# Ten codebook levels parted around block sums, and one square moved behind a bank's copy

## The chip, the cores and the metric

The kernel runs on one core of a Trainium2 chip. The metric is the device time in microseconds (us) from one launch; three timed runs of the kernel before gave 1450.16, 1450.33 and 1450.46 us, with a median of 1450.33. The profile comes from one further execution that took 1451.06 us. Its span, from the first to the last instruction, is 1449.3 us, so 1.8 us lie around the span.

## The reference

The input x has 64 rows of 32 tokens with 512 features. What matters here:

```
W = weights[condition]                      # one of 16 mixing matrices for each of the 64 rows
hidden = einsum('bct,bcd->bdt', x, W)
q = rms_norm(hidden @ Wq + bq, gq)          # 512 -> 4096, 32 heads of 128
k = rms_norm(hidden @ Wk + bk, gk)
v = hidden @ Wv + bv
x = x + softmax(q k^T / sqrt(128)) v @ Wo + bo      # attention within each row's 32 tokens
lora_delta = lora_B @ lora_A * 0.5
normalized = (weight + lora_delta) / exp(scale_log)          # 512 x 512, groups of 128
quantized = cb[searchsorted((cb[:-1] + cb[1:]) / 2, normalized)]   # 64 codes
w_eff = (quantized - normalized + normalized) * scale + lora_delta
x = x + mixture_of_8_low_rank_experts(x @ w_eff.T)
```

The norm needs the sum of squares of q and of k over all 4096 features of a token. The quantised weight is looked up without a table: for each of the 63 thresholds ("levels") it adds step[t] wherever normalized > threshold[t].

## The kernel before, in words

All products are float32 in quality, made from float32r parts: an operand is kept as a rounded part (hi) and a rest (lo), and a product is hi\*hi + hi\*lo + lo\*hi, three matmuls for each 128 rows of depth.

**The q and k stage** is the first half of the program and the only one that the change touches. For each of 32 heads it makes q and k for two halves of the tokens, so there are 64 instances, counted by s (head h = s // 2; N_QK = 64). An instance is one Strassen-like block product: seven products (`p1` to `p7` of the TensorE part, line 720) stand for eight. Each is 6 matmuls of 512 columns. The order on TensorE is p6(s), p5(s), p1(s+1), p7(s), the scores of the head before where s is even (128 small matmuls, line 848), p2(s+1), p4(s), p3(s). I call p3 the third product and p4 the fourth, by their numbers. p3(s) adds into the bank that p5(s) filled, and it may only start once the result k_hi has been read out of that bank.

**ScalarE** copies intermediate banks to SBUF (`keep_a1`, `keep_a2`, `keep_a3`, lines 1166, 1175, 1184), rounds the weights (`split_qk`, line 1105), squares each of the four results of an instance (`square`, lines 1196 and 1198), scales q (`gain`, line 1202) and copies p4's bank out as k_lo (line 1284). The bank of p4(s) is also the one of p1(s+2); p1(s+2) waits for `sq_ready` to reach `sq_k_lo(s)`, that is for the square which reads this bank. The count of `sq_ready` follows the order of the squares on ScalarE: q_lo, k_hi, k_lo, q_hi.

**VectorE** makes the four results of an instance as block sums of a bank and a kept copy: `block_11` (q_lo, line 1761), `block_22` (k_hi, line 1774), `block_12` (q_hi, line 1787), each 128x512. It makes the rests of the weights (`low_qk`, line 1623), copies the scores out (`keep_scores`, line 1746), and between them walks the levels of the codebook for the first half of the weight. One level is two instructions of 128x1024: a comparison (line 1727, into qm) and a sum into qf (line 1728). The function `levels_qk(s)` gives 1 level to instances 6 to 59, and 2 to instances 7, 13, 19, ..., 55. The first level of an instance stands ahead of `block_22(s)`, the second near its end, ahead of `block_12(s)`.

**GpSimd** adds the squares to their running sums (`add_square`, line 1526, 128x512; the first 8 squares go there directly) and forms sums of weight blocks (`add_qk`, lines 1477 to 1489, 128x256).

The order on every engine is the order in which the code is written; engines meet by semaphores alone. A helper `link` makes VectorE wait for its own instruction before it goes on. After this stage come the v stage (line 739), attention and output projection (lines 922 and 963), and the experts. The change leaves them as they are.

Of the kernel before, what the change touches and what calls it, by code (L numbers as in the profile page):

```python
# [8 lines left out]
ALU = mybir.AluOpType  # L9
# [71 lines left out]

def levels_qk(s):
    return 0 if s < 6 or s > 59 else 2 if s > 6 and s % 6 == 1 else 1


def levels_v(s):
# [25 lines left out]
def build(nc, x_nat, x_tr, cond_w, cond_idx, codebook, wqk, wv_in, wo_in, vecs, bo, w2, scale_log,  # L112
# [4 lines left out]
    with ExitStack() as ctx:  # L117
        def sb(name, shape, dt=F32):
            return ctx.enter_context(nc.sbuf_tensor(name, shape, dt))

        def sem(name):
            return ctx.enter_context(nc.semaphore(name))
# [9 lines left out]
        thr = sb("thr", [P, NCODE + 1])  # L132
        thr_t = sb("thr_t", [P, NCODE])
        step = sb("step", [P, NCODE])
# [29 lines left out]
        with ExitStack() as mem_a:  # L164
# [29 lines left out]
        blk = {(name, par): qk[:, (2 * i + par) * 512:(2 * i + par + 1) * 512]  # L194
               for i, name in enumerate(("q_lo", "q_hi", "k_lo", "k_hi")) for par in range(2)}
# [5 lines left out]
        qv = (qreg[:, 0:1024], accr[:, 0:1024])  # L201
        update = (qreg[:, 1024:2048], accr[:, 2048:3072])
        qf = (qreg[:, 2048:3072], accr[:, 1024:2048])
        qm = qreg[:, 3072:4096]
# [53 lines left out]
        def bank_a(s):  # L258
            return bank[4 - 4 * (s % 2)]
# [90 lines left out]
        c22_done = sem("c22_done")  # L350
# [57 lines left out]
        def sq_q_lo(s):  # L408
            return 4 * s + 1

        def sq_k_hi(s):
            return 4 * s + 2

        def sq_k_lo(s):
            return 4 * s + 3

        def sq_q_hi(s):
            return 4 * s + 4
# [4 lines left out]
        def sq_slot(count):  # L423
            return sqst[:, (count - 1 - SQ_DIRECT) % 3, :]

        def acc_of(kind, n):
            return acc[:, kind, n * CH:(n + 1) * CH]
# [659 lines left out]
        def _(act):  # L1087
# [100 lines left out]
            def square(count, kind, n, src, bias):  # L1188
                if count <= SQ_DIRECT:
                    dst = acc_of(kind, n)  # L1190
                else:
                    if count > SQ_DIRECT + 3:
                        act.wait_ge(acc_done, count - SQ_DIRECT - 3)
                    dst = sq_slot(count)
                if bias is None:
                    act.activation(dst, src, ACT.Square).then_inc(sq_ready, 1)  # L1196
                else:
                    act.activation(dst, src, ACT.Square, bias=bias, scale=1.0).then_inc(sq_ready, 1)

            def gain(name, s, ready):  # L1200
                q = blk[name, s % (3 if name == "q_lo" else 2)]
                act.activation(q, q, ACT.Copy, scale=vec[:, s // 2, 3:4]).then_inc(ready, 1)

            def last_q(s):

                act.wait_ge(c12_done, s + 1)
                square(sq_q_hi(s), 0, s % 2 + 2, blk["q_hi", s % 2], None)
# [40 lines left out]
            for s in range(N_QK):  # L1248
                if s >= 1:
                    keep_a2(s)  # L1250
                    last_q(s - 1)
                    gain("q_hi", s - 1, gq_hi)
                if s == 2:
                    split_qk(4, 2)
                if s == 1:
                    keep_a3(s)
                act.wait_ge(c11_done, s + 1)
                square(sq_q_lo(s), 0, s % 2, blk["q_lo", s % 3], None)
                gain("q_lo", s, gq_lo)
                h = s // 2  # L1260
                if s % 2 == 1 and h + 1 < H:
                    split_qk(6, h + 1)
                elif s % 2 == 0 and s >= 2:
                    split_qk(3, h)
                if s >= 2:
                    keep_a3(s)
                elif s == 0:
                    difference(3, 7)
                if s % 2 == 1 and h + 1 < H:
                    split_qk(7, h + 1)  # L1270
                if s == N_QK - 1:
                    split_v(5, 0)
                    split_v(6, 0)
                keep_a1(s + 1)
                if s == 0:
                    split_qk(1, 1)
                    difference(2, 4)
                    difference(3, 4)
                act.wait_ge(c22_done, s + 1)
                square(sq_k_hi(s), 1, s % 2 + 2, blk["k_hi", s % 2], None)  # L1280
                if s % 2 == 0 and s >= 2 and h + 1 < H:
                    split_qk(1, h + 1)
                act.wait_ge(p_done[4], s + 1)
                act.activation(blk["k_lo", s % 2], bank_a(s)[:, :], ACT.Identity, bias=vec[:, h, 1:2], scale=1.0)\
                   .then_inc(c21_done, 1)
                square(sq_k_lo(s), 1, s % 2, bank_a(s)[:, :], vec[:, h, 1:2])
                if s == 0:
                    split_qk(4, 1)
                elif s % 2 == 1:
                    if s > 1 and h + 2 < H:  # L1290
                        split_qk(4, h + 2)
                if s == N_QK - 2:
                    split_v(1, 0)
                    split_v(2, 0)
# [308 lines left out]
        def _(dve):  # L1603
            chained = [0]

            def link(ins):
                chained[0] += 1
                ins.then_inc(chain, 1)
                dve.wait_ge(chain, chained[0])
# [37 lines left out]
            def code_order(s, last):  # L1647
                while s >= last:
                    mid, low, high = thr[:, s:NCODE:2 * s], thr[:, 0:NCODE:2 * s], thr[:, 2 * s:NCODE + 1:2 * s]
                    link(dve.tensor_tensor(mid, mid, low, ALU.max))  # L1650
                    link(dve.tensor_tensor(mid, mid, high, ALU.min))
                    s //= 2
# [70 lines left out]
            def first_level(half):  # L1723
                link(dve.tensor_scalar(qf[half], qv[half], 0.0, cb[:, 0:1], ALU.mult, ALU.add))

            def level(half, t):
                link(dve.tensor_scalar(qm, qv[half], thr[:, t + 1:t + 2], step[:, t:t + 1], ALU.is_gt, ALU.mult))
                link(dve.tensor_tensor(qf[half], qf[half], qm, ALU.add))  # L1728

            def straight_through(half, steps=(0, 1)):  # L1730
                for step in steps:
# [92 lines left out]
            taken = 0  # L1824
            for s in range(N_QK):
                h = s // 2
                if s >= 2:
                    block_12(s - 1)
                if s == 2:
                    low_qk(4, 2)  # L1830
                if s == 3:
                    code_steps()
                if s == 4:
                    normalised(0)
                if s == 5:
                    code_order(NCODE // 2, NCODE // 8)
                if s == 2:
                    dve.wait_ge(t_lo, 16)
                    code_scales(0)
                if s == 6:  # L1840
                    first_level(0)
                if s == 60:
                    straight_through(0)
                if s == 61:
                    effective(0)
                if levels_qk(s):
                    level(0, taken)
                    taken += 1
                if s == 1:
                    block_22(s)  # L1850
                if s % 2 == 1 and h + 1 < H:
                    low_qk(6, h + 1)
                elif s % 2 == 0 and s >= 2:
                    low_qk(3, h)
                if s == N_QK - 1:
                    low_v(1, 0)
                    low_v(2, 0)
                if s >= 2:
                    block_22(s)
                if s % 2 == 0 and s >= 2:  # L1860
                    keep_scores(s // 2 - 1)
                if s % 2 == 1 and h + 1 < H:
                    low_qk(7, h + 1)
                if s + 1 < N_QK:
                    block_11(s + 1)
                if s == 3:
                    keep_update(0)
                    keep_update(1)
                    dve.wait_ge(ld_quant[0], 16)
                if s == 4:  # L1870
                    normalised(1)
                if s == 5:
                    code_order(NCODE // 16, 1)
                if levels_qk(s) == 2:
                    level(0, taken)
                    taken += 1
                if s == N_QK - 1:
                    low_v(5, 0)
                if s == 0:
                    low_qk(1, 1)  # L1880
                    block_12(s)
                    low_qk(4, 1)
                elif s % 2 == 1:
                    if s > 1 and h + 2 < H:
                        low_qk(4, h + 2)
                elif h + 1 < H:
                    low_qk(1, h + 1)
                if s == 2:
                    code_scales(1)
# [70 lines left out]
            taken = 0  # L1960
# [217 lines left out]
```

## Time and profile before

| | |
|---|---|
| median of 3 runs | 1450.33 us (1450.16 to 1450.46) |
| the profiled execution | 1451.06 us, span 1449.3 us |
| TensorE busy | 1444.4 us of the span, 14507 matmuls |
| VectorE, ScalarE, GpSimd busy | 1080.4, 726.0, 745.2 us |
| granted TensorE clock | 1.0 |
| line 720, the products of the q and k stage | 2688 matmuls, from 13.6 to 682.4 us |
| a level of the first half: comparison, sum | 1199 ns and 1650 ns on the mean, 63 of each |
| block_22 (line 1774) | 688 ns on the mean, 96 of them |

A busy TensorE only says that some matmul was under way. A late start shows there as a longer pair of matmuls or as a gap ahead of a weight load, which the profile lists on its own row as PEld. The chain that ended last is made of TensorE's work for 98%.

### The profile page before, as it was taken

What the parts mean: (1) busy time and instruction counts of PE and PEld (TensorE: products, weight loads), DVE (VectorE), ACT (ScalarE), POOL (GpSimd) and SP (SyncE); (2) the same over time, 40 slices, a digit from 0 to 9 for tenths busy, and PEclk for the clock granted to TensorE, in tenths of its full rate; (3) what the DMA queues carried; (4) which work ended last, traced back from release to release, by engine and by line L of the source; (5) the groups of instructions that cost most, each with busy time, mean ns of one, the idle gap of its engine ahead of it and who ended that gap; (6) DMA issues with size and microseconds to landing.
All of it is one profiled execution on the core that took longest, in us unless ns stands there. A gap on an engine that the chain in (4) does not pass through costs nothing.

```text
span 1449.3 us, 34721 instructions
## 1 busy us (share of the span) xinstructions
PE 1444.4 (100%) x14507; PEld 1200.5 (83%) x14507; DVE 1080.4 (75%) x1507; ACT 726.0 (50%) x1331; POOL 745.2 (51%) x530
## 2 busy tenths in 40 slices
PE   9999999999999999999999999999999999999999
PEld 8788888888888888888888888888888888888887
DVE  8787868687786877875478888867987667667663
ACT  7766676766766767677333333334432322222221
POOL 7568777777777877776345555514561111112100
PEclk9999999999999999999999999999999999999999
DMA  4211011110111011102443344447663334244230
GB/s 152 66 45 45 31 38 45 45 45 24 45 45 45 27 41 45 45 31 67 136 152 139 133 133 137 145 148 246 201 194 110 103 118 132 83 137 132 74 118 30
DMA packets 106989, 135.13 MB, mean 93 GB/s; under 512 B 6224, under 2 KB 89424, under 8 KB 106320
## 3 DMA queue, kind: packets, MB, share of 16 engines
q1 hardware_dynamic: 106400, 132.62, 27.7%
q8 instruction: 114, 1.87, 0.5%
q14 instruction: 43, 0.35, 0.1%
q10 hardware_dynamic: 432, 0.30, 0.1%
HBM read 86.75 MB, written 46.14 MB: 92 GB/s over the span
## 4 chain that ended last, share of the span: by engine, by line
PE 98%; DVE 1%; issue 0%; ACT 0%; DVEq 0%; POOL 0%; ACTq 0%; POOLq 0%
PE bank L720 41%; PE bank L963 25%; PE bank L739 21%; PE bank L922 4%; PE bank L848 3%; PE bank L991 1%; PE bank L1009 1%; PE bank L669 0%; DVE wa L1623 0%; PE bank L648 0%; PE bank L977 0%; PE bank L1020 0%; DVE xs_lo L1685 0%; DVE sqst L1707 0%; PE bank L1041 0%
## 5 line engine op out<-in xcount | busy, mean ns | idle before, releaser
L720 PE MATMUL bank<-xs_hi,wa 128*128 128x512 f32 x1792 | 563.9, 392 | 0.0
L1526 POOL TENSOR_TENSOR accr<-accr,sqst 128x512 f32<-128x512 f32 x248 | 351.9, 1429 | 149.7 <-ACT sqst L1196 109.9
L720 PEld LDWEIGHTS bank<-xs_hi,wa 128*128 128x128 f32 x1792 | 336.3, 188 | 74.5 <-DVE qk L1774 2.4
L720 PE MATMUL bank<-xs_lo,wa 128*128 128x512 f32 x896 | 349.0, 390 | 0.0
L963 PE MATMUL bank<-ot,wo_main 128*128 128x512 f32 x1344 | 316.4, 392 | 0.0
L963 PEld LDWEIGHTS bank<-ot,wo_main 128*128 128x128 f32 x1344 | 249.6, 188 | 52.5
L739 PE MATMUL bank<-wv,xs_hi 128*128 128x512 f32 (+1 forms) x1008 | 282.6, 366 | 0.1
L1623 DVE TENSOR_TENSOR wa<-wraw,wa 128x256 fp32r<-128x256 f32 (+1 forms) x160 | 159.4, 997 | 96.2 <-ACT wa L1105 94.3
L1321 ACT ACTIVATE ot<-bank,vec 128x256 fp32r<-128x256 f32 x256 | 100.2, 475 | 240.4 <-PE bank L963 146.5
L739 PEld LDWEIGHTS bank<-wv,xs_hi 128*128 128x128 f32 x1008 | 182.1, 189 | 32.8 <-issue 1.9
L720 PEld LDWEIGHTS bank<-xs_lo,wa 128*128 128x128 f32 x896 | 168.3, 188 | 33.6
L1954 DVE SCALAR_TENSOR_TENSOR ot<-bank,vec,ot 128x256 fp32r<-128x256 f32 x256 | 106.1, 477 | 114.0 <-ACT ot L1321 113.5
L739 PE MATMUL bank<-wv,xs_lo 128*128 128x512 f32 (+1 forms) x504 | 184.2, 365 | 0.0
L1569 POOL TENSOR_TENSOR wraw<-wraw,rinv 128x1024 f32<-128x1024 f32 x16 | 32.5, 2033 | 273.5 <-DVE rinv L1936 273.5
L1774 DVE TENSOR_TENSOR qk<-bank,snap 128x512 f32<-128x512 f32 x96 | 66.1, 688 | 94.6 <-ACT snap L1186 60.7
L1196 ACT ACTIVATE sqst<-qk 128x512 f32<-128x512 f32 x165 | 103.5, 627 | 63.0 <-DVE qk L1774 39.7
L1948 DVE STREAM_TRANSPOSE weights_b<-wraw 32x256 f32<-32x256 f32 x256 | 111.4, 435 | 3.5
L739 PEld LDWEIGHTS bank<-wv,xs_lo 128*128 128x128 f32 x504 | 95.0, 189 | 15.3
L1728 DVE TENSOR_TENSOR qreg<-qreg 128x1024 f32<-128x1024 f32 x63 | 103.9, 1650 | 2.2
L1728 DVE TENSOR_TENSOR accr<-accr,qreg 128x1024 f32<-128x1024 f32 x63 | 100.8, 1600 | 2.2
L1105 ACT ACTIVATE wa<-wraw 128x256 fp32r<-128x256 f32 (+1 forms) x160 | 79.0, 495 | 3.6 <-PE bank L720 3.6
L1175 ACT ACTIVATE snap<-bank,vec 128x512 f32<-128x512 f32 x64 | 44.2, 691 | 72.4 <-PE bank L720 72.4
(224 smaller groups left out, 1724.5 us busy)
## 6 DMA issues: line engine op xcount, KB each, us to landing
values_b<-v_spill SPq DMA_DIRECT2D x60, 512.0 KB, 4.9
wraw<-in_wqk SPq DMA_DIRECT2D x32, 512.0 KB, 3.5
v_spill<-qk SPq DMA_DIRECT2D x64, 256.0 KB, 2.3
v_spill<-sqst SPq DMA_DIRECT2D x64, 256.0 KB, 2.1
score_spill<-sqst SPq DMA_DIRECT2D x32, 256.0 KB, 2.0
wraw<-in_wv SPq DMA_DIRECT2D x16, 512.0 KB, 5.1
wraw<-score_spill SPq DMA_DIRECT2D x16, 512.0 KB, 4.0
spare<-in_wo SPq DMA_DIRECT2D x15, 512.0 KB, 4.9
```

Source lines behind the costliest of these rows:

```text
L720: ins = pe.matmul(dst[:, :], wa[:, col:col + P], xpart[:, j - 1, kt, n * CH:(n + 1) * CH], start=(first and k == 0), stop=(k == 5), skip_g ...
L739: ins = pe.matmul(out, xpart[:, j - 1, kt, t * P:(t + 1) * P], rhs, start=(first and k == 0), stop=(k == last), skip_group_check=True)
L963: ins = pe.matmul(bank[i][:, :], wo_slot(p)[:, wpart, col:col + P], ot[:, b % 2, opart, h, :], start=(p == 0 and k == 0), stop=(p == NP - ...
L1105: act.activation(wa[:, col:col + n], wraw[:, src:src + n], ACT.Copy).then_inc(w_hi[g], 1)
L1196: act.activation(dst, src, ACT.Square).then_inc(sq_ready, 1)
L1321: ins = act.activation(ot_part(ot[:, b % 2, 0, h, :], r), pv_part(b, r, h), ACT.Identity, bias=vec[:, 2 * (b % NP) + h, 2:3], scale=1.0)
L1526: pool.tensor_tensor(a, a, sq_slot(count), ALU.add).then_inc(acc_done, 1)
L1623: dve.tensor_tensor(wa[:, col + n:col + 2 * n], wraw[:, src:src + n], wa[:, col:col + n].bitcast(F32), ALU.subtract).then_inc(w_lo[g], 1)
L1728: link(dve.tensor_tensor(qf[half], qf[half], qm, ALU.add))
L1774: dve.tensor_tensor(dst, bank_b(s)[:, :], a3, ALU.add).then_inc(c22_done, 1)
L1948: ins = dve.transpose(pt[rows, b % 2, :, :, j * C:(j + 1) * C], src)
L1954: ins = dve.scalar_tensor_tensor(out=ot_part(ot[:, b % 2, 1, h, :], r), in0=pv_part(b, r, h), scalar=vec[:, 2 * (b % NP) + h, 2:3], in1=ot ...
```

## The change

There are two edits.

1. A level is split into `level_step` (the comparison) and `level_sum`. In the ten instances 6, 8, 14, 20, 26, 32, 38, 44, 50 and 56 (`level_split`) the comparison stays where it was, and the sum goes behind `low_qk(3)`, `block_22(s)`, `keep_scores` and `block_11(s + 1)`; it then stands ahead of `low_qk(1)` and `block_12(s)`.
2. In instance 0 ScalarE copies and squares the bank of the fourth product (k_lo) first, and squares k_hi behind it. The numbers that stand for these two squares are exchanged for s = 0.

```diff
+def level_split(s):
+    return s == 6 or 6 < s < 60 and s % 6 == 2
...
         def sq_k_hi(s):
-            return 4 * s + 2
+            return 4 * s + 2 if s else 3
         def sq_k_lo(s):
-            return 4 * s + 3
+            return 4 * s + 3 if s else 2
...
-                act.wait_ge(c22_done, s + 1)
-                square(sq_k_hi(s), 1, s % 2 + 2, blk["k_hi", s % 2], None)
+                if s >= 1:
+                    act.wait_ge(c22_done, s + 1)
+                    square(sq_k_hi(s), 1, s % 2 + 2, blk["k_hi", s % 2], None)
                 if s % 2 == 0 and s >= 2 and h + 1 < H:
                     split_qk(1, h + 1)
                 act.wait_ge(p_done[4], s + 1)
                 act.activation(blk["k_lo", s % 2], bank_a(s)[:, :], ACT.Identity, bias=vec[:, h, 1:2], scale=1.0)\
                    .then_inc(c21_done, 1)
                 square(sq_k_lo(s), 1, s % 2, bank_a(s)[:, :], vec[:, h, 1:2])
+                if s == 0:
+                    act.wait_ge(c22_done, s + 1)
+                    square(sq_k_hi(s), 1, s % 2 + 2, blk["k_hi", s % 2], None)
...
+            def level_step(half, t):
+                link(dve.tensor_scalar(qm, qv[half], thr[:, t + 1:t + 2], step[:, t:t + 1], ALU.is_gt, ALU.mult))
+            def level_sum(half):
+                link(dve.tensor_tensor(qf[half], qf[half], qm, ALU.add))
...
                 if levels_qk(s):
-                    level(0, taken)
+                    level_step(0, taken)
                     taken += 1
+                    if not level_split(s):
+                        level_sum(0)
...
                 if s == 5:
                     code_order(NCODE // 16, 1)
+                if level_split(s):
+                    level_sum(0)
                 if levels_qk(s) == 2:
                     level(0, taken)
```

On VectorE the stretch from `block_12(7)` to `block_12(8)` reads so before (a number behind a bank is the bank's; line 1727 is the comparison, 1728 the sum, 1623 `low_qk`, 1774 `block_22(8)`, 1746 `keep_scores`, 1761 `block_11(9)`):

```order
L1787 TENSOR_TENSOR qk<-bank1,snap 128x512
L1727 TENSOR_SCALAR qreg<-qreg,thr,step 128x1024
L1728 TENSOR_TENSOR qreg<-qreg 128x1024
L1623 TENSOR_TENSOR wa<-wraw,wa 128x256
L1774 TENSOR_TENSOR qk<-bank5,snap 128x512
L1746 COPY sqst<-bank3 128x512
L1761 TENSOR_TENSOR sqst<-bank2,snap 128x512
L1623 TENSOR_TENSOR wa<-wraw,wa 128x512
L1787 TENSOR_TENSOR qk<-bank5,snap 128x512
```

The same stretch of the changed kernel, whose lines have moved (1735 is the comparison, 1738 the sum, 1631 `low_qk`, 1788, 1760, 1775 and 1801 the others in their order):

```order
L1801 TENSOR_TENSOR qk<-bank1,snap 128x512
L1735 TENSOR_SCALAR qreg<-qreg,thr,step 128x1024
L1631 TENSOR_TENSOR wa<-wraw,wa 128x256
L1788 TENSOR_TENSOR qk<-bank5,snap 128x512
L1760 COPY sqst<-bank3 128x512
L1775 TENSOR_TENSOR sqst<-bank2,snap 128x512
L1738 TENSOR_TENSOR qreg<-qreg 128x1024
L1631 TENSOR_TENSOR wa<-wraw,wa 128x512
L1801 TENSOR_TENSOR qk<-bank5,snap 128x512
```

The sum has gone down four rows; nothing is added or taken away.

On ScalarE, around the end of instance 0, before (1196 is a square of SBUF, 1284 the copy of the fourth product's bank, 1198 the square of that bank):

```order
L1159 ACTIVATE xs_hi<-qreg 128x512
L1196 ACTIVATE accr<-qk 128x512
L1284 ACTIVATE qk<-bank,vec 128x512
L1198 ACTIVATE accr<-bank,vec 128x512
L1105 ACTIVATE wa<-wraw 128x256
```

And of the changed kernel (1163, 1289, 1202, 1200 and 1109 stand for 1159, 1284, 1198, 1196 and 1105):

```order
L1163 ACTIVATE xs_hi<-qreg 128x512
L1289 ACTIVATE qk<-bank,vec 128x512
L1202 ACTIVATE accr<-bank,vec 128x512
L1200 ACTIVATE accr<-qk 128x512
L1109 ACTIVATE wa<-wraw 128x256
```

The square of k_hi has gone behind the two instructions that read the bank. TensorE, GpSimd and the DMA queues keep their order.

## Rows read from the trace of the kernel before

**Rows 1.** The page: busy time and share of the span

```profile
PE 1444.4 (100%) x14507; PEld 1200.5 (83%) x14507; DVE 1080.4 (75%) x1507; ACT 726.0 (50%) x1331; POOL 745.2 (51%) x530
```

**Rows 2.** Waits of TensorE and its weight loads: us in total, times, longest

```profile
PE bank L848 <- ACT qk L1202: 0.3, 1, 0.3
...
PEld bank L720 <- DVE qk L1774: 2.4, 10, 0.4
...
PEld bank L720 <- ACT accr L1198: 0.5, 1, 0.5
```

**Rows 3.** The chain that ended last: start us, us, what

```profile
72.43 19.29 PE bank L720 x84
92.95 5.99 PE bank L720 x24
114.06 19.37 PE bank L720 x84
...
299.01 19.36 PE bank L720 x84
319.60 19.29 PE bank L720 x84
...
607.34 19.39 PE bank L720 x84
```

**Rows 4.** Timeline of TensorE's matmuls: start us, us, merged instructions

```profile
36.42 0.92 PE L720 MATMUL bank<-xs_hi,wa 128*128 128x512 f32 x2
...
311.18 0.62 PE L720 MATMUL bank<-xs_hi,wa 128*128 128x512 f32 x2
```

**Rows 5.** Timeline of TensorE's weight loads, instance 26

```profile
301.77 0.19 PEld L720 LDWEIGHTS bank<-xs_hi,wa 128*128 128x128 f32 x1 [0.20 <-DVE qk L1774]
```

**Rows 6.** Timeline of VectorE, instances 25 to 28

```profile
292.37 2.34 DVE L1728 TENSOR_TENSOR qreg<-qreg 128x1024 f32<-128x1024 f32 x1
...
295.50 0.68 DVE L1787 TENSOR_TENSOR qk<-bank,snap 128x512 f32<-128x512 f32 x1
296.11 1.33 DVE L1727 TENSOR_SCALAR qreg<-qreg,thr,step 128x1024 f32<-128x1024 f32 x1
...
299.70 1.41 DVE L1623 TENSOR_TENSOR wa<-wraw,wa 128x256 fp32r<-128x256 f32 x1
301.04 0.68 DVE L1774 TENSOR_TENSOR qk<-bank,snap 128x512 f32<-128x512 f32 x1
...
302.94 1.37 DVE L1623 TENSOR_TENSOR wa<-wraw,wa 128x512 fp32r<-128x512 f32 x1
...
306.04 1.23 DVE L1728 TENSOR_TENSOR qreg<-qreg 128x1024 f32<-128x1024 f32 x1
308.39 1.84 DVE L1623 TENSOR_TENSOR wa<-wraw,wa 128x512 fp32r<-128x512 f32 x1 [1.12 <-ACT wa L1105]
...
315.05 0.80 DVE L1727 TENSOR_SCALAR qreg<-qreg,thr,step 128x1024 f32<-128x1024 f32 x1
```

**Rows 7.** Timeline of GpSimd, instances 25 to 27

```profile
292.33 1.29 POOL L1526 TENSOR_TENSOR accr<-accr,sqst 128x512 f32<-128x512 f32 x1 [0.55 <-ACT sqst L1198]
...
296.93 3.90 POOL L1526 TENSOR_TENSOR accr<-accr,sqst 128x512 f32<-128x512 f32 x2
...
302.46 1.29 POOL L1526 TENSOR_TENSOR accr<-accr,sqst 128x512 f32<-128x512 f32 x1 [0.46 <-ACT sqst L1196]
...
306.10 3.58 POOL L1526 TENSOR_TENSOR accr<-accr,sqst 128x512 f32<-128x512 f32 x2 [0.64 <-ACT sqst L1196]
```

**Rows 8.** Timeline of ScalarE, instances 26 to 28

```profile
296.21 0.63 ACT L1196 ACTIVATE sqst<-qk 128x512 f32<-128x512 f32 x1 [1.81 <-DVE qk L1787]
...
298.50 0.40 ACT L1105 ACTIVATE wa<-wraw 128x256 fp32r<-128x256 f32 x1
...
305.39 0.62 ACT L1196 ACTIVATE sqst<-qk 128x512 f32<-128x512 f32 x1
...
322.60 0.69 ACT L1284 ACTIVATE qk<-bank,vec 128x512 f32<-128x512 f32 x1 [0.69 <-PE bank L720]
```

More of the change, by code:

```diff
@@ L1724, in first_level @@
                 link(dve.tensor_scalar(qf[half], qv[half], 0.0, cb[:, 0:1], ALU.mult, ALU.add))
+            def level_step(half, t):
+                link(dve.tensor_scalar(qm, qv[half], thr[:, t + 1:t + 2], step[:, t:t + 1], ALU.is_gt, ALU.mult))
+            def level_sum(half):
+                link(dve.tensor_tensor(qf[half], qf[half], qm, ALU.add))
             def level(half, t):
-                link(dve.tensor_scalar(qm, qv[half], thr[:, t + 1:t + 2], step[:, t:t + 1], ALU.is_gt, ALU.mult))
-                link(dve.tensor_tensor(qf[half], qf[half], qm, ALU.add))
+                level_step(half, t)
+                level_sum(half)
             def straight_through(half, steps=(0, 1)):
```

## The prediction

> **What bounds the kernel.** I read the page first. TensorE is busy for 1444.4 of 1449.3 us [rows 1], so a change on VectorE or ScalarE can give only what TensorE waits for them, and it can take as much as it makes TensorE wait. The list of waits comes next [rows 2]. The weight loads of line 720 waited ten times for `block_22` (line 1774), never over 0.4 us, and once for the square of the fourth product's bank (line 1198); the scores waited once for a scaled q (line 1202). The chain gives what this costs [rows 3]: two instances without a wait take 92.95 - 72.43 = 20.52 us. The pair 299.01 to 319.60 takes 20.59, and the pair from 92.95 to 114.06 takes 21.11. The timelines come last [rows 4 to 8], for instance 26, one of the ten, and instance 27.
>
> **What can be gained.** In instances 8, 14, ..., 56 the piece of 84 matmuls that ends with the third product lasts 19.36 to 19.41 us where the others last 19.29 (the first, the 299.01 one and the last of the nine are shown) [rows 3]; together they are 0.81 us over. The pair from 92.95 is 0.59 over; 0.31 of that is the scores' wait in instance 8 [rows 2], and 0.28 is instance 6. In instance 0 a pair of matmuls took 0.92 where 0.62 is usual (0.62 stands at 311.18) [rows 4]: 0.30. The second edit moves the awaited square forward by one square (0.52 or more: a square lasts 0.62 and the next one starts 0.10 before its end), and the wait was 0.45 to 0.5, so the 0.30 goes. The square of k_hi that takes the late place, and the weight rounding behind both, end when they did before. The first edit puts `block_22` ahead of a sum that took over a microsecond, so 0.81 + 0.28 goes too. The gain is 1.4 us. Nothing is added: ten sums of 128x1024 change place, with no DMA and no queue of SyncE.
>
> **What the move costs.** A sum that leaves early room must use late room. I follow instance 26. VectorE's instructions with two SBUF inputs and GpSimd's adds exclude each other here: the two adds at 296.93 take 3.90 us, a lone one 1.29 [rows 7], and the rest pass at 299.70 ends 301.11, 0.28 after them; the one at 308.39 ends 310.23, 0.55 after two adds that end 309.68 [rows 6, 7]. Block sums, which read a bank, keep 0.68.
>
> - The comparison ends 297.44 as before [rows 6]. `low_qk(3)` is now next, but its rounded part is ready at 298.90 on ScalarE [rows 8]; with the 0.11 from there to VectorE (as in instance 27, where the rounding ends 3.00 after 305.39 less that lag) it asks at 299.01. VectorE has stood still for 1.5 us. GpSimd's first add ends about 298.6 and its second, no longer stopped by the sum, at 299.86. `low_qk(3)` ends 0.28 later, 300.14.
> - `block_22` runs 300.07 to 300.75, where it ended 301.72. TensorE's load went at 301.77 [rows 5], so this wait is gone with 0.9 to spare.
> - 1.90 after `block_22`'s start (301.04 to 302.94 [rows 6]) the sum stands at 301.97. GpSimd's add of the k_hi square started 0.74 after `block_22`'s end (301.72 to 302.46) [rows 6, 7], now 301.49, and holds until 302.78. The sum ends 1.08 after it (292.37 + 2.34 = 294.71, against an add that ends 293.62), at 303.86.
> - The fourth product's copy starts 3.00 after the piece behind the scores (322.60 against 319.60) [rows 3, 8]: 302.01. Its square follows 0.57 later, and GpSimd asks for the add at 303.35, before the sum's end; it is served next, until 305.02 (an add ends 1.15 after a sum that it waited for: 306.04 + 1.23 = 307.27, and the pair at 306.10 ends 309.68, less one add of 1.29). `low_qk(1)` ends 0.55 later, 305.57, and `block_12(26)` starts 305.49. Before, it started at 304.24, just before the end of 302.94 + 1.37. So VectorE goes into instance 27 late by 1.25 us.
>
> In instance 27 this meets the next free stretch, the 1.12 us that VectorE waited ahead of 308.39 [rows 6]. ScalarE's square of q_hi starts 0.71 after `block_12` (295.50 to 296.21) [rows 6, 8] at 306.20, and GpSimd wants its add at 306.91. The comparison starts 0.61 after `block_12`, takes 0.80 when nothing is in its way (315.05), and the sum of instance 27 wants to start at 306.92 to 306.95. The two come within 0.04 us of each other. Two rows lie on either side: the add at 292.33 is 0.04 ahead of the sum at 292.37, and the sum took 2.34; the sum at 306.04 is 0.06 ahead of the add at 306.10 and took 1.23 [rows 6, 7]. The estimate, 0.01 to 0.04 ahead for the add, is nearest to the first, so I let the add go first. Then the add ends 308.20, the sum 309.28, the next add, which has waited, 310.43, and `low_qk(6)` 310.98. `block_22(27)` ends 311.59.
>
> The Trainium skill ("SBUF — State Buffer", section "Who interferes with whom") says that an exclusive lock is held for a whole instruction and that whoever issues first gets it. The lone durations above agree. By it a sum that comes first leaves instance 27 without a wait, which is the first rival below.
>
> TensorE's third product of instance 27 started at 311.41, the second of the pair at 311.18 [rows 4], now 311.35. In instance 26 a `block_22` that ended 301.72 cost 0.07, which puts the free point about 0.18 ahead of the product's first matmul: the cost is 311.59 - 311.35 + 0.18 = **0.42 us**. Its bounds are 0 (the order of add and sum the other way) and 0.9 (should ScalarE's third kept copy be late as well). It falls nine times, in instances 9, 15, ..., 57: 3.8 us.
>
> Instance 6 goes the same way (its two adds at the start end 93.7 in place of squeezing the sum), and instance 7 gets 0.36. Instance 7 has two levels, so the delay stays: its `block_12` is about 0.45 later against TensorE, and the scores of instance 8, which wait for q_hi of 7, wait 0.76 in place of 0.31. That is 0.8 more.
>
> **Sum.** 3.8 + 0.8 - 1.4 = +3.2 us. The profiled execution would come to 1451.06 + 3.2 = 1454.3 (span 1452.5), and the median of the runs, 0.7 below the profiled one, to **1453.5 us**. With 0.42 uncertain by 0.12 each time, this case's own range is 1452.3 to 1454.8.
>
> **Rivals.**
>
> *The sum goes first (faster).* Place: instance 27 and its like. Decided by 0.01 to 0.04 us. The sum runs 306.92 to 308.15 and the add ends 309.30; `low_qk(6)` asks at 309.20, 3.00 after the square, 0.07 before the second add would begin; it runs to 309.85 and `block_22(27)` ends 310.46, early. No new wait anywhere, and instance 7, whose `block_22` then comes sooner than before, lets the scores of 8 go 0.28 sooner. Time: 1450.33 - 1.4 - 0.3 = 1448.6. For it: TensorE has no other wait in these instances; the sum at 306.04 did win by 0.06. Against it: the estimate has the wrong sign.
>
> *Mixed.* The order of add and sum is settled anew in each period (they differ by hundredths), or the wait is half as long, since VectorE comes in 0.2 us earlier than I made it. With three to six waits of 0.4 the two ends nearly cancel: 1450.0 to 1452.2, no change. For it: a margin of 0.01 to 0.04. Against it: the nine pieces of the chain repeat within 0.05 us (19.36 to 19.41).
>
> *Worse.* The rest pass of instance 27 loses to yet another add, or `keep_a3(27)`, which stands behind the late square of q_hi on ScalarE, makes the fourth product wait too. Another 0.3 us nine times: 1456. Little speaks for it, since no third square is ready by then.
>
> *It doesn't do what it says.* `low_qk(3)` cannot start before 299.01, but `block_22` still ends 0.97 us sooner, and the wait was 0.2. I give this no chance of its own.
>
> **Numbers.** Forecast 0.45, the sum first 0.28, mixed 0.19, worse 0.08. What a measurement of this kernel can tell from no change is taken as 0.2%, 2.9 us: the lines are 1447.4 and 1453.2. The forecast lies just past the upper one, so some 0.6 of it counts as slower (0.27), with all of the worse case (0.08): 0.35. Faster by 2.9 us is out of reach of a gain of 1.7: 0.02. The rest, 0.63, is no change. The range from 1448.4 to 1454.8 takes in the first rival and the mixed case and leaves out the worse one and the upper end of the forecast.
>
> **What the next profile would show.** The waits of line 720's loads for `block_22` would stand at ten again, or at ten with longer times, near 0.5 us, but in instances 7, 9, 15, ..., 57. In instance 26 the rest pass would follow a gap of 1.5 us, `block_22` would end near 300.7 relative to the same start, and the moved sum would take about 1.9 us. In instance 27 the sum would last 2.3 us rather than 1.23. The wait for line 1198 would be gone. If instead that sum lasts 1.2 us and the odd instances take 9.5 us without a wait, the first rival holds. I am wrong on the gain if the pair 299.01 to 319.60 stays at 20.59.

## The result: 3 us slower, and where they lie in the profile after

The changed kernel takes 1453.4 us (median of 12 runs, 1452.59 to 1454.12), the kernel before 1450.41 (median of 12 runs too). The ratio is 1.0022 (95% interval 1.0014 to 1.003). The forecast was 1453.5.

The profiled span grew from 1449.3 to 1452.2 us. The page after, against [rows 1]:

```profile
PE 1446.4 (100%) x14507; PEld 1200.4 (83%) x14507; DVE 1088.9 (75%) x1507; ACT 726.4 (50%) x1331; POOL 738.6 (51%) x530
```

The waits of TensorE and its weight loads after (us in total, times, longest; the lines have moved by 4 on TensorE, 1788 is `block_22`, 1631 `low_qk`, 1206 the scaled q), against [rows 2]:

```profile
PE bank L852 <- ACT qk L1206: 0.7, 1, 0.7
...
PEld bank L724 <- DVE qk L1788: 4.9, 10, 0.5
PEld bank L724 <- DVE wa L1631: 1.7, 9, 0.2
```

There are ten waits for `block_22` again, twice as long, and they are no longer the same ten. The wait for line 1198 is gone. Nine waits for `low_qk` are new. Because matmuls overlap, the cost is best read as the distance between the first matmuls of p6 in successive instances, which I took from TensorE's timeline:

```
us of one instance          before    after    (other even: 19 instances, 2, 4, 10, 12, ..., 58)
instance 1                    9.92     9.57
instance 6                   11.29    10.95
instance 7                    9.52     9.94
instance 8                   11.38    11.75
14, 20, ..., 56 (mean of 8)  11.11    11.01
9, 15, ..., 57 (mean of 9)    9.53     9.94
other even                   10.99    10.96
other odd (without 3)         9.52     9.52
```

Instance 3 holds one more product and is left out. The instances whose level was parted got shorter, all but instance 8, whose scores wait for a result of 7. The instances behind them got longer by more. VectorE in instances 26 and 27 (timeline: start us, us, instruction; 1735 is the comparison, 1738 the sum, 1801 `block_12`), against [rows 6]:

```profile
297.55 1.33 DVE L1735 TENSOR_SCALAR qreg<-qreg,thr,step 128x1024 f32<-128x1024 f32 x1
300.45 1.11 DVE L1631 TENSOR_TENSOR wa<-wraw,wa 128x256 fp32r<-128x256 f32 x1 [1.57 <-ACT wa L1109]
301.48 0.68 DVE L1788 TENSOR_TENSOR qk<-bank,snap 128x512 f32<-128x512 f32 x1
...
303.27 2.00 DVE L1738 TENSOR_TENSOR qreg<-qreg 128x1024 f32<-128x1024 f32 x1
305.31 1.66 DVE L1631 TENSOR_TENSOR wa<-wraw,wa 128x512 fp32r<-128x512 f32 x1
306.89 0.68 DVE L1801 TENSOR_TENSOR qk<-bank,snap 128x512 f32<-128x512 f32 x1
307.50 0.80 DVE L1735 TENSOR_SCALAR qreg<-qreg,thr,step 128x1024 f32<-128x1024 f32 x1
308.33 2.37 DVE L1738 TENSOR_TENSOR qreg<-qreg 128x1024 f32<-128x1024 f32 x1
310.73 1.67 DVE L1631 TENSOR_TENSOR wa<-wraw,wa 128x512 fp32r<-128x512 f32 x1
312.33 0.68 DVE L1788 TENSOR_TENSOR qk<-bank,snap 128x512 f32<-128x512 f32 x1
```

GpSimd beside it, against [rows 7]:

```profile
302.90 1.29 POOL L1534 TENSOR_TENSOR accr<-accr,sqst 128x512 f32<-128x512 f32 x1 [0.46 <-ACT sqst L1200]
304.80 1.63 POOL L1534 TENSOR_TENSOR accr<-accr,sqst 128x512 f32<-128x512 f32 x1 [0.61 <-ACT sqst L1202]
308.32 3.53 POOL L1534 TENSOR_TENSOR accr<-accr,sqst 128x512 f32<-128x512 f32 x2 [1.90 <-ACT sqst L1200]
```

Read them together. In 26 VectorE stands still for 1.57 us ahead of `low_qk(3)`. The parted sum at 303.27 meets the add at 302.90 and ends 1.08 behind it. `low_qk(1)` meets the next add. In 27 the add starts at 308.32 and the sum at 308.33: the sum waits it out and takes 2.37 us where it took 1.23 before. It is the same in all ten instances 7, 9, 15, ..., 57: the add starts 6 to 13 ns ahead of the sum, and the sum takes 2.37 to 2.38; in the kernel before the sum was ahead by 56 to 112 ns each time. The next add then holds up `low_qk(6)`, and `block_22(27)` ends at 313.01. TensorE's load stands right behind it (against [rows 5]):

```profile
313.06 0.19 PEld L724 LDWEIGHTS bank<-xs_hi,wa 128*128 128x128 f32 x1 [0.49 <-DVE qk L1788]
```

Earlier in the same walk stands a wait that I had not foreseen, of the first load of p1(28), for `low_qk(1, 14)`, which ended at 306.97 (305.31 + 1.66):

```profile
307.02 0.30 PEld L724 LDWEIGHTS bank<-xs_hi,wa 128*128 128x128 f32 x2 [0.18 <-DVE wa L1631]
```

### The profile page after: what moved, and what is told of

It reads as the page before. It is cut to its first block, busy times and chain, and to the rows that moved or that the text cites. A ratio compares the mean times of both kernels' runs of the same rounds, so it can differ in the third digit from the quotient of the medians.

```text
span 1452.2 us, 34731 instructions
## 1 busy us (share of the span) xinstructions
PE 1446.4 (100%) x14507; PEld 1200.4 (83%) x14507; DVE 1088.9 (75%) x1507; ACT 726.4 (50%) x1331; POOL 738.6 (51%) x530
## 4 chain that ended last, share of the span: by engine, by line
PE 93%; ACT 3%; DVE 2%; issue 1%; DVEq 0%; ACTq 0%; POOL 0%; POOLq 0%
PE bank L724 37%; PE bank L967 24%; PE bank L743 21%; PE bank L926 4%; PE bank L852 3%; ACT qk L1206 1%; PE bank L995 1%; PE bank L1013 1%; DVE qk L1801 1%; ACT wa L1109 1%; ACT snap L1179 0%; DVE qk L1788 0%; PE bank L673 0%; ACT snap L1170 0%; ACT sqst L1200 0%
## 5 line engine op out<-in xcount | busy, mean ns | idle before, releaser
L1534 POOL TENSOR_TENSOR accr<-accr,sqst 128x512 f32<-128x512 f32 x248 | 345.8, 1407 | 159.9 <-ACT sqst L1200 121.9
L1631 DVE TENSOR_TENSOR wa<-wraw,wa 128x256 fp32r<-128x256 f32 (+1 forms) x160 | 162.4, 1016 | 96.8 <-ACT wa L1109 95.0
L1738 DVE TENSOR_TENSOR qreg<-qreg 128x1024 f32<-128x1024 f32 x63 | 113.4, 1800 | 1.8
```

The costliest lines, as they stand in the source:

```text
L1534: pool.tensor_tensor(a, a, sq_slot(count), ALU.add).then_inc(acc_done, 1)
L1631: dve.tensor_tensor(wa[:, col + n:col + 2 * n], wraw[:, src:src + n], wa[:, col:col + n].bitcast(F32), ALU.subtract).then_inc(w_lo[g], 1)
```

## Experiments

Times are medians beside runs of the kernel before on the same chip; the ratios carry their 95% intervals. Where there is a single run, there is one time and no interval. The kernel before took 1450.93, 1450.31 or 1451.1 beside them, and the expected times were reckoned from about 1450.3, so the difference to the kernel before says more than the time itself.

### Each edit alone

The square alone, with `level_split` returning False:

```diff
 def level_split(s):
-    return s == 6 or 6 < s < 60 and s % 6 == 2
+    return False
```

> The second edit alone; no level is parted. Port theory (the moved sums collide with GpSimd's adds in the odd instances): only the first wait goes, 0.3 us faster than before, about 1450.1, with nine waits of 0.2 us for block_22 in instances 8, 14, ..., 56 and one in 6 still there. Rival (the exchange of the two squares, or the moved code, costs what the change cost): 1452 to 1453.

1450.77 us against 1450.93, ratio 0.9999 (0.999 to 1.0007). Instances 6, 8 and 14 to 56 are as before (11.30, 11.36, 11.11), and so are the waits for `block_22` (2.6 us, 11 times). Instance 1 went from 9.92 to 9.69; in the changed kernel it took 9.57, and this profile has two short waits for another operand in its place (`xs_lo`, 0.4 us together). A gain of 0.2 to 0.3 us shows in the trace alone, since the interval of the times is wider than it. No cost of the edit shows.

The parting alone, with the squares of instance 0 as before:

```diff
-            return 4 * s + 2 if s else 3
+            return 4 * s + 2
...
-            return 4 * s + 3 if s else 2
+            return 4 * s + 3
...
-                if s >= 1:
-                    act.wait_ge(c22_done, s + 1)
-                    square(sq_k_hi(s), 1, s % 2 + 2, blk["k_hi", s % 2], None)
+                act.wait_ge(c22_done, s + 1)
+                square(sq_k_hi(s), 1, s % 2 + 2, blk["k_hi", s % 2], None)
...
-                if s == 0:
-                    act.wait_ge(c22_done, s + 1)
-                    square(sq_k_hi(s), 1, s % 2 + 2, blk["k_hi", s % 2], None)
```

> The first edit alone; instance 0 as before. Port theory: 3.0 + 0.3 over before, about 1453.7, with instances 7, 9, 15, ..., 57 each 0.42 us over 9.52 and the scores of 8 waiting 0.76. Rival (the exchange of squares costs it): 1450.

1454.67 us against 1450.93, ratio 1.0025 (1.0016 to 1.0035), instances 9, 15, ..., 57 at 9.96 and instance 7 at 9.93. That is 3.7 us more than before where I expected 3.3; the interval takes in both. The whole loss is the first edit's.

### The order of one add and one sum

Nothing changes on VectorE here; GpSimd does one tiny thing more.

```diff
                 if s >= 1:
+                    if s == 7 or s >= 9 and s % 6 == 3:
+                        pool.wait_ge(sq_ready, sq_q_hi(s - 1))
+                        pool.memset(scratch[:, (s - 3) // 6:(s + 3) // 6], 0.0)
                     add_square(sq_q_hi(s - 1), 0, (s - 1) % 2 + 2)
```

> The changed kernel, with one more instruction on GpSimd, a memset of one column, between the wait for the q_hi square of instances 6, 8, 14, ... and its add. It delays the add by a tenth or two, so that the sum of instances 7, 9, 15, ... is first. Port theory: that sum takes 1.23 in place of 2.37 us, low_qk(6) takes less than 1, block_22 of the odd instances ends over 1 us sooner, no wait for it is left, and the scores of 8 go on time: 1448.8 to 1449.6, although VectorE does the same work in the same order. Rival (VectorE is late in the odd instances because the parted level left a hole, and the order of add and sum does not matter): 1453.4, unchanged.

1449.85 us against 1450.93, ratio 0.9993 (0.9984 to 1.0002): 3 us and more below the changed kernel, whose interval (1.0014 to 1.003) it does not touch. The time is 0.25 above the upper end of what I expected; by the difference to the kernel before (1.1 us less) it lies inside. Instances 9, 15, ... take 9.59, instance 7 9.58 and instance 8 11.00. VectorE in instance 27 (line 1739 the comparison, 1742 the sum, 1635 `low_qk`, 1792 `block_22`):

```profile
305.40 0.80 DVE L1739 TENSOR_SCALAR qreg<-qreg,thr,step 128x1024 f32<-128x1024 f32 x1
306.23 1.23 DVE L1742 TENSOR_TENSOR qreg<-qreg 128x1024 f32<-128x1024 f32 x1
308.51 0.69 DVE L1635 TENSOR_TENSOR wa<-wraw,wa 128x512 fp32r<-128x512 f32 x1 [1.06 <-ACT wa L1110]
309.12 0.68 DVE L1792 TENSOR_TENSOR qk<-bank,snap 128x512 f32<-128x512 f32 x1
```

GpSimd beside it:

```profile
306.20 0.10 POOL L1543 MEMSET scratch<- 128x1 f32 x1 [1.87 <-ACT sqst L1201]
306.29 4.07 POOL L1535 TENSOR_TENSOR accr<-accr,sqst 128x512 f32<-128x512 f32 x2
```

The memset lasts 0.10 us. The add now starts 0.06 behind the sum instead of 0.01 ahead of it; the sum takes 1.23 in place of 2.37, and `low_qk(6)` 0.69 in place of 1.67, because it in turn starts before the second add. `block_22` ends 4.40 us after the comparison starts (309.80 - 305.40), where in the changed kernel it took 5.51 (313.01 - 307.50). The list of waits has none for `block_22` left; the nine for `low_qk` are still there, 1.7 us with their usual gaps:

```profile
PEld bank L725 <- DVE wa L1635: 1.7, 9, 0.2
```

VectorE is as late against TensorE as in the changed kernel: the comparison of instance 27 starts 2.91 us after TensorE's instance does, there 2.88, in the kernel before 1.58. So this lateness costs only the 0.06 us of `low_qk(1)` by itself. The rival falls.

The control puts the same ten memsets into the kernel before, where the sum is first anyway.

```diff
                 if s >= 1:
+                    if s == 7 or s >= 9 and s % 6 == 3:
+                        pool.wait_ge(sq_ready, sq_q_hi(s - 1))
+                        pool.memset(scratch[:, (s - 3) // 6:(s + 3) // 6], 0.0)
                     add_square(sq_q_hi(s - 1), 0, (s - 1) % 2 + 2)
```

> A control: the kernel before with the same ten memsets ahead of the q_hi adds of instances 7, 9, 15, ..., 57. There the sum is first anyway, by 0.06 us, and the second add starts when the first one ends, so nothing should move: the time of before within 0.5 us, instances 9, 15, ... 9.53. If the memset speeds the kernel up by another way (a rival for what it did to the changed kernel), it should be 1 us or more faster than before here too.

1451.17 against 1451.1, ratio 1.0001 (0.9992 to 1.001), instances 9, 15, ... at 9.53. The memset does nothing of its own there.

Instance 6 took 11.02 in this profile and 11.29 in the first one of the kernel before, though the first memset comes later. The first place where the two profiles part is another near tie, in instance 5: a `low_qk` of 128x256 and an add of weight blocks start at 88.38 and 88.37 in the kernel before, and the `low_qk` takes 1.00 us; here both start at 88.63, the add 5 ns ahead, and yet `low_qk` takes 0.43 and the add 1.04. In the other eleven profiles the add was 7 to 10 ns ahead and went first. So a tie this close can fall either way. That instance 6 went with it is read from the order of events, and no run shows it by itself.

### A short add

```diff
-                a = acc_of(kind, n)
-                pool.tensor_tensor(a, a, sq_slot(count), ALU.add).then_inc(acc_done, 1)
+                a, b = acc_of(kind, n), sq_slot(count)
+                if count % 4 == 0 and level_split(count // 4 - 1):
+                    a, b = a[:, 0:16], b[:, 0:16]
+                pool.tensor_tensor(a, a, b, ALU.add).then_inc(acc_done, 1)
```

> The changed kernel, but GpSimd adds only 16 of the 512 columns of the q_hi squares of instances 6, 8, 14, ..., 56; the rest of these sums is left out of the result. Port theory: the sum of instances 7, 9, 15, ... still starts 0.01 us behind this add, but the add holds the port for some 0.1 to 0.2 us, so the sum takes under 1.5, and instances 9, 15, ... take at most 9.6 us in place of 9.94. A rival that has nothing to do with the length of the add: 9.94 stays.

This kernel leaves out the rest of ten squares, so its result is of no use, only its time. One run: 1449.52 us against 1450.31, 9.59 in instances 9, 15, ... Here the add still comes 0.01 us first, at 306.03 against 306.04, and lasts 0.22. GpSimd's add, then VectorE:

```profile
306.03 0.22 POOL L1536 TENSOR_TENSOR accr<-accr,sqst 128x16 f32<-128x16 f32 x1 [1.89 <-ACT sqst L1200]
...
306.04 1.29 DVE L1740 TENSOR_TENSOR qreg<-qreg 128x1024 f32<-128x1024 f32 x1
308.32 0.71 DVE L1633 TENSOR_TENSOR wa<-wraw,wa 128x512 fp32r<-128x512 f32 x1 [0.99 <-ACT wa L1109]
```

The order is that of the changed kernel; what counts is how long the first of the two holds the second up.

### Which instances share the loss

```diff
-    return s == 6 or 6 < s < 60 and s % 6 == 2
+    return 8 < s < 60 and s % 6 == 2
```

> The changed kernel with levels parted in 14, 20, ..., 56 alone. My sum gave 0.8 us to instances 7 and 8 together: instance 6 should be back at 11.29, 7 at 9.52, 8 at 11.37 with the scores' wait back at 0.3, and 9 at 9.53, while 15, 21, ... keep 9.94. A rival in which the periods hang together (a late period makes the next one late) would move 14 and 15 too.

One run: 1452.6 us against 1450.31. Instances 6, 7, 8 take 11.30, 9.52 and 11.36, as before the change; 15, 21, ..., 57 take 9.94. The periods don't hang together, and instances 6 to 8 carry their own part: 10.95 + 9.94 + 11.75 = 32.64 with the change and 32.18 without.

### Two other places for the work

First the parted sum behind `block_12` of its instance:

```diff
                 if s >= 2:
                     block_12(s - 1)
+                if level_split(s - 1):
+                    level_sum(0)
...
-                if level_split(s):
-                    level_sum(0)
```

> The changed kernel, but the ten sums stand behind low_qk(1) and block_12(s) of their instance too, at the head of the next. Port theory: block_12(26) comes 1.4 us sooner, so does the square of q_hi and its add, and the moved sum falls into the free stretch ahead of low_qk(6) of the odd instance; block_22(27) ends within 0.1 us of the free point, and low_qk(1) no longer makes p1 wait: 1449.0 to 1449.8. Rival (any place behind block_22 makes the odd instance late by a sum of over 1 us, since VectorE's work is the same): 1453 or more.

1450.16 against 1450.93, ratio 0.9994 (0.9985 to 1.0003). Instances 9, 15, ... take 9.54 and the waits for `low_qk(1)` are gone. The time is 0.4 above the upper end of what I expected, though by the difference to the kernel before (0.8 less) it lies inside. Without a miss in instance 8 it would have been lower by 0.7: that instance takes 11.67, for the scores wait 0.6 us:

```profile
PE bank L852 <- ACT qk L1206: 0.6, 1, 0.6
```

Instance 7 has two levels of its own; a third sum at its head pushes its `block_12` back. That I had not worked out.

Then the parting kept in 8, 14, ..., 56, and the whole level of instances 9, 15, ..., 57 moved behind `block_11(s + 1)`:

```diff
+def level_late(s):
+    return 8 < s < 60 and s % 6 == 3
...
-                if levels_qk(s):
+                if levels_qk(s) and not level_late(s):
                     level_step(0, taken)
...
+                if level_late(s):
+                    level(0, taken)
+                    taken += 1
```

> Levels parted in 8, 14, ..., 56 (not in 6), and in instances 9, 15, ..., 57 the whole level stands behind block_11(s + 1), so that nothing of 128x1024 stands between block_12 and low_qk(6). Port theory: low_qk(6) meets only the two adds, block_22 of the odd instances is on time (9.52 to 9.6, with 0.06 left for low_qk(1)), the pairs lose the waits of 8, 14, ..., and 6 to 8 stay as before: 1449.4 to 1450.2. If lateness as such is what counts, the level moved back makes the next even instance late and the time stays over 1452.

1451.79 against 1450.31, ratio 1.001 (1.0001 to 1.002). A miss: I expected up to 1450.2. Instances 9, 15, ... were cured (9.60), but 10, 16, ... went to 11.17. In instance 28 `block_22` ends at 322.32 (in the kernel before at 320.43, and TensorE is at about the same point in both), and ten waits are back, most of them two instances behind the parted ones. VectorE in instance 28 (1742 the sum, 1635 `low_qk`, 1792 `block_22`):

```profile
318.10 2.19 DVE L1742 TENSOR_TENSOR qreg<-qreg 128x1024 f32<-128x1024 f32 x1
320.32 1.40 DVE L1635 TENSOR_TENSOR wa<-wraw,wa 128x256 fp32r<-128x256 f32 x1
321.64 0.68 DVE L1792 TENSOR_TENSOR qk<-bank,snap 128x512 f32<-128x512 f32 x1
```

Its waits of weight loads:

```profile
PEld bank L728 <- DVE qk L1792: 2.3, 10, 0.4
```

Of the 0.2 us that instances 10, 16, ... lose, half lies in the stretch with the scores (2.79 in place of 2.68) and most of the rest in the third product (1.44 in place of 1.36). A level behind `block_11` makes the next `block_12` late (316.14 against 314.45), with a level of the next instance right behind that. The rival, that a level moved back makes the next even instance late, holds for this place in kind; its time, over 1452, was not reached either.

### The two cures together

```diff
                 if s >= 2:
                     block_12(s - 1)
+                if s > 7 and level_split(s - 1):
+                    level_sum(0)
...
-                if level_split(s):
+                if s == 6:
                     level_sum(0)
...
                 if s >= 1:
+                    if s == 7:
+                        pool.wait_ge(sq_ready, sq_q_hi(s - 1))
+                        pool.memset(scratch[:, 0:1], 0.0)
                     add_square(sq_q_hi(s - 1), 0, (s - 1) % 2 + 2)
```

> The two cures together: from instance 8 on the parted sum stands behind block_12(s), in instance 6 it stands where the change puts it, and the add of instance 7 is delayed by one memset. Port theory: 6, 7 and 8 take 10.95, 9.58 and 11.0 us, 9, 15, ... 9.54: 1449.3 to 1449.8, 0.3 to 0.5 below the add delayed everywhere (1449.85). The rival says that the two cures work by different causes and don't add: 1449.9 or more.

1448.68 against 1450.31, ratio 0.9989 (0.998 to 0.9998): faster than both kernels. Instances 6, 7 and 8 take 10.95, 9.57 and 11.01, and 9, 15, ... 9.54. The gain over before is 1.6 us, and the time is 0.6 below the lower end of what I expected. The interval reaches to 0.9998, so its size is not well known. The rival, that the cures don't add, named 1449.9 or more. Against the kernels before beside them the cures alone gained 1.1 and 0.8 us, with intervals that overlap this one's; in the traces the 61 instances from 1 to 61 take 626.5 and 627.2 us with one cure and 626.0 with both. In the first profile of the kernel before they take 628.3, 2.3 more than with both, 0.7 of which is the matter of the next run.

### The kernel before, once more

This run has no edit.

> The kernel before, word for word, profiled once more. In the profile of before the even instances without a wait take 10.99 us, in most of the changed ones 10.95, with no edit near them. If this 0.04 belongs to the program, it stays 10.99; if it belongs to the execution, it may be 10.95 here.

One run: 1450.98 us, span 1449.2. The other even instances take 10.95 here, against 10.99 in the first profile. So these 0.04 us, 0.7 over 19 instances, belong to the execution. The start moves as well: instance 1 begins at 33.88 in the first profile and at 34.45 here, as in the changed kernel.

## Why the prediction was right

**The bound and the gain.** TensorE is the bound in both, and only its waits moved. The gain was put at 1.4 us: 0.30 for the square, 0.28 for instance 6 and 0.81 for nine third products. The trace after gives 0.34 for instance 1 and 0.33 for instance 6 (0.04 of it the execution's; and instance 6 came down to 11.02 once without this edit, in the control's profile). The third products of 8, 14, ... have the usual 1.36 us after, 1.45 before. For the square it is shown by the edit alone, in the trace and not in the time. One sign that I had named can't be read as I wrote it: the pair of instances that took 20.59 takes 20.93 after, because it ends behind the scores of 28 and takes in the loss of 27. With both cures it takes 20.51.

**The hole in VectorE.** It was put at 1.5 us ahead of `low_qk(3)`; it is 1.57. From its comparison's start, `low_qk(3)` ended 4.03 after in the working (296.11 to 300.14) and 4.01 in the trace, and `block_12(26)` started 9.38 after in the working (305.49) and 9.34 in the trace. Of the steps between, none was off by more than 0.1 us, except the start of the moved sum, which came 0.14 earlier than worked out and had to wait for the add all the same.

**The order of add and sum.** Put at 0.01 to 0.04 us for the add, measured 0.01 in instance 27 and the nine others; the sum took 2.37. That this decides is shown: 0.1 us more on GpSimd takes the whole loss away (1449.85), a short add does the same (1449.52), and the same 0.1 us does nothing where the sum is first. The first rival was the right account of the other branch. It put it 1.7 us below the kernel before, and with the add delayed it was 1.1 below: the rival left out the wait for `low_qk(1)`, 0.06 us ten times. That the sign came out right rests on a margin as narrow as a hundredth of a microsecond, which the prediction said; it was the likelier branch and not a safe one.

**The size of the wait.** Put at 0.42 nine times, it is 0.41, but it is made of two. The fourth and the third product, between which TensorE waits for `block_22`, took 0.36 more together, and p5(s) with the p1(s + 1) behind it 0.06. This second part was missing from my working: I took `low_qk(1)` to be in no hurry, but p1(s + 1) already runs in instance s, so that p1(28) needs in instance 27 what `low_qk(1, 14)` makes at the end of 26. The total came out right because the two don't add: `block_22(27)` ended 0.24 behind the free start of the third product, counted from the instance's start, in the working and in the trace alike, and what TensorE had already lost to `low_qk(1)` it did not lose again here. With the add delayed, where the later wait is gone, the 0.06 stands alone (9.59 against 9.53).

**Instances 7 and 8.** Put at 0.36 and 0.45; measured 0.42 and 0.42 (the scores' product with its wait went from 2.99 to 3.41 us). Shown by leaving 6 and 8 whole.

**The sum.** Forecast +3.2 and measured 3.0 by the medians, 2.9 by the spans. That the spans agree so well is in part luck: the first profile of before had 0.7 us more in its even instances and 0.6 less in its start than the one after, and the two nearly cancel. The second profile of before has the even instances and the start of the one after, and against it the span grew by 3.0 (1449.2 to 1452.2). The medians of twelve runs average over both. With the lines that the prediction drew for what can be told from no change, 1453.2 above, the measured 1453.4 lies just past the line, on the side to which it had given 0.35 and not 0.63.

What stays open: what decides between an add and a sum that start almost together was only seen at the distances that came up, and no run varied it in steps. The add went first whenever it was 6 ns or more ahead, the sum whenever it was 56 ns or more ahead, and nothing was seen between; the one case at 5 ns, of a `low_qk` and a GpSimd add, went against the recorded order.

## To carry to other kernels

When TensorE is full, a wait of 0.1 us on its list may be removed only by work that has somewhere to go: follow the moved instruction until its engine next stands idle, one instance further than seems needed, and count as a cost the hole that it leaves where the next instruction isn't ready. Where VectorE and GpSimd work on SBUF at once, write both timelines side by side and look for starts within a tenth of a microsecond; there the cheapest edit may be a delay on the engine that has time. And for every weight that a pass makes, look up in which instance its product really runs.

## What the runs showed of the hardware

- VectorE's `tensor_tensor` with two SBUF inputs and GpSimd's `tensor_tensor` held each other up for the whole of an instruction. With the add 0.01 us ahead of the sum (308.32 and 308.33) the sum ended 1.08 us behind the end of an add of 1.29, and with the add 0.06 us behind (306.29 and 306.23) the sum took its lone 1.23. `tensor_scalar` of 128x1024 float32 was held up too: 0.80 alone, 1.33 where an add of 128x256 ran beside it (297.55). The Trainium skill ("SBUF — State Buffer", section "Who interferes with whom") has it that whoever issues first gets the pair for the whole instruction. By the recorded starts these runs agree for sums and adds down to 6 ns. They don't for the comparison: at 90.69 in the kernel before it started 0.04 us ahead of a GpSimd add of 1.29 us (90.73), and took 1.88 us, so that it ended 0.55 behind the add. The recorded start of a comparison is then not the moment that decides.
- A GpSimd memset of 128x1 took 0.10 us, and the sum beside it (306.20 and 306.23) its lone 1.23.
- In two executions of the kernel before, TensorE's even instances took 10.99 and 10.95 us, and instance 1 began at 33.88 and 34.45 us. Ahead of it 32 small matmuls took 1.37 us in the first and 1.94 in the second.
